# Four paths of low-rank weights per sequence on one core: one visit to z, y, tokens and o per turn of four pairs in place of two visits of two

## The reference

```python
x = x + L0(x)   # x W_base^T + (((x Wt^T) A[e0]^T) B_w[e0]^T) Wp^T * scaling[e0]     e0 of 4, rank 16
x = x + L1(x)   # x W^T + (x A[e1]^T) Bm[e1]^T * scalings[e1]                        e1 of 8, rank 16
x = x + L2(x)   # einsum('bct,bcd->bdt', x, weights[e2]): mixes the 64 tokens        e2 of 8
x = x + L3(x)   # the same with 200 sets of 64x64 weights                            e3 of 200
```

## Time and profile before

| | us |
|---|---|
| median of 3 runs (lowest, highest) | 200.63 (199.47, 202.59) |
| the profiled execution | 200.97 |
| its span, first to last instruction | 199.1 |
| TensorE busy in it | 177.4 |
| the eight turns, from the first z to the end of the last o | 48.7 to 195.6 |

### The profile page before, as it was taken

How to read it: one execution, slowest core, us unless ns; L and a number is a source line. 1 busy time by engine, 2 the same in 40 slices (tenths; PEclk the granted TensorE clock), 3 DMA queues, 4 the chain that set the end, 5 groups by cost and what they waited for, 6 DMA issues and landing times.

```text
span 199.1 us, 7261 instructions
## 1 busy us (share of the span) xinstructions
PE 177.4 (89%) x2304; PEld 140.1 (70%) x2304; DVE 96.8 (49%) x232; ACT 94.2 (47%) x183; POOL 71.7 (36%) x184
## 2 busy tenths in 40 slices
PE   6599898696889699999898989898898989999992
PEld 6377574575668487878686867777686868787781
DVE  1288588629653651746074527524650646154210
ACT  2365742126336645455463636354544545564521
POOL 2525787030653056306521741373056303113000
PEclk9999999999999999999999999999999999999999
DMA  3999412222372846375555737482847375443412
GB/s 80 394 357 289 155 46 87 53 66 72 84 262 71 266 151 198 87 245 164 179 168 173 248 84 229 119 259 78 256 121 229 99 232 169 151 162 82 180 72 89
DMA packets 19081, 32.39 MB, mean 163 GB/s; under 512 B 5878, under 2 KB 5878, under 8 KB 19062
## 3 DMA queue, kind: packets, MB, share of 16 engines
q1 hardware_dynamic: 17744, 31.11, 50.0%
q0 software_dynamic: 1024, 1.05, 1.8%
q10 hardware_dynamic: 294, 0.01, 0.1%
HBM read 22.98 MB, written 9.18 MB: 162 GB/s over the span
## 4 chain that ended last, share of the span: by engine, by line
PE 59%; issue 11%; DVE 9%; ACT 9%; DVEq 6%; DMA 2%; another core or an unknown queue 1%; POOL 0%; SPq 0%; ACTq 0%
PE o_ps L733 35%; PE y_ps L733 8%; PE z_ps L733 5%; DVE y_all L619 4%; PE spare_ps L733 4%; PE p_ps L733 3%; ACT yy L444 3%; DVEq L667 3%; DVEq L657 2%; DMA w_sb<-in_L_cond_W_dram 2%; DVE w_sel L667 2%; ACT z L477 1%; ACT v_sel L458 1%; PE y_ps L745 1%
## 5 line engine op out<-in xcount | busy, mean ns | idle before, releaser
L733 PE MATMUL o_ps<-g,yy 128*128 128x512 f32 x384 | 95.2, 396 | 0.0
L733 PEld LDWEIGHTS o_ps<-g,yy 128*128 128x128 f32 x384 | 70.8, 188 | 16.2
L340 POOL COPY u_sel<-u_tab 128x64 f32 x128 | 28.0, 242 | 89.8 <-PE z_ps L733 70.1
L330 POOL DMA_INDIRECT w_all<-in_L_cond_weights_dram,w_rows x32 | 31.7, 990 | 12.8 <-issue 9.7
L465 ACT ACTIVATE o_sb<-o_ps 128x512 f32<-128x512 f32 x32 | 19.2, 599 | 33.8 <-PE o_ps L733 32.4
L444 ACT ACTIVATE yy<-y_all 128x512 fp32r<-128x512 f32 x32 | 19.6, 635 | 25.4 <-DVE y_all L619 21.5
L633 DVE TENSOR_TENSOR z_sum<-z_ps,z_half 64x128 f32<-64x128 f32 x16 | 4.5, 282 | 50.4 <-ACT z_half L472 50.4
L626 DVE TENSOR_TENSOR yy<-y_all,yy 128x512 fp32r<-128x512 f32 x32 | 20.7, 690 | 2.9 <-ACT yy L444 1.9
L619 DVE COPY y_all<-y_ps 128x512 f32<-128x512 f32 x32 | 20.6, 686 | 0.5
L733 PE MATMUL o_ps<-v_sel,z 128*128 128x512 f32 x64 | 20.1, 394 | 0.0
L733 PE MATMUL z_ps<-y_all,u_sel 128*32 128x64 f32 x512 | 11.6, 222 | 9.4 <-DVE w_sel L667 5.1
(11 more groups left out here) (124 smaller groups left out, 139.8 us busy)
## 6 DMA issues: line engine op xcount, KB each, us to landing
x_raw<-in_x_dram SPq DMA_DIRECT2D x16, 512.0 KB
v_sel<-v_table SPq DMA_DIRECT2D x128, 64.0 KB, 2.1
out_dram<-o_sb SPq DMA_DIRECT2D x14, 512.0 KB, 3.1
w_sb<-in_L_cond_W_dram SPq DMA_DIRECT2D x4, 256.0 KB, 4.8
wb_sb<-in_L_cond_W_base_dram SPq DMA_DIRECT2D x4, 256.0 KB, 6.3
wp_sb<-in_L_cond_Wp_dram SPq DMA_DIRECT2D x2, 512.0 KB, 6.8
wt_sb<-in_L_cond_Wt_dram SPq DMA_DIRECT2D x1, 1024.0 KB
out_dram<-o_sb SPq DMA_DIRECT2D x4, 256.0 KB, 2.8
```

The costliest lines, as they stand in the source:

```text
L330: pool.indirect_dma_start(out=w3_all[:, j, :], out_offset=None, in_=w3_flat, in_offset=bass.IndirectOffsetOnAxis(ap=w3_rows[:, j:j + 1], a ...
L340: nc.gpsimd.tensor_copy(u_sel[u % 2][:, :, b, RANK * part:RANK * part + RANK], u_tab[:, :, bass.ds(e, 1), :].rearrange("p k a r -> p k (a r)")
L733: return nc.tensor.matmul(dst, lhsT, rhs, start=start, stop=stop)
```

## The change

TensorE makes one visit a turn: `reduce(i)` (z of four pairs), `mix()` (y of the four pairs of turn i+1), `token_mix(i+2)`, then four applies. All its waits but those of apply stand at the head: `mix_ready(i+1)`, `token_ready(i+2)`, then those of reduce. y_ps has four banks, y_all, u_sel and z are for four pairs. The keep-warm transposes and three setup products use the new banks of y_ps.

```diff
-        y_ps = ctx.enter_context(nc.psum_tensor("y_ps", [PART, 2, D], F32))
+        y_ps = ctx.enter_context(nc.psum_tensor("y_ps", [PART, QUAD, D], F32))
...
-                 "g01_0": 6, "g01_1": 4, "g01_2": 5, "g01_3": 7}
+                 "g01_0": 6, "g01_1": 4, "g01_2": 5, "g01_3": 1}
```

SyncE, one turn, and GpSimd:

```diff
+            def turn(i, loads=True):
                 if loads:
-                    load(i + 1 + h, 1 - h)
-                for u in range(2 * h, 2 * h + 2):
-                    fetch_v(i + 1, u)
-                store(i, h)
+                    for h in range(2):
+                        load(i + 2, h)
+                for h in range(2):
+                    for u in range(2 * h, 2 * h + 2):
+                        fetch_v(i + 1, u)
+                    store(i, h)
...
-            for u in range(2):
+            for u in range(QUAD):
                 place_u(0, u)
...
+            gather_w3(range(2 * QUAD, 3 * QUAD))
+
+            for i in range(QUADS - 1):
+                if i < QUADS - 3:
+                    pool.wait_ge(w3_plus, i + 3)
+                    gather_w3(range(QUAD * (i + 3), QUAD * (i + 4)))
+
+                pool.wait_ge(z_done, i + 1)
+                for u in range(QUAD):
+                    place_u(i + 1, u)
```

ACT, with V doubled in the turn that uses it:

```diff
+            def turn(i, first=False, ahead=True, more=True):
+                act.wait_ge(z_done, i + 1)
...
+                if ahead and not first:
+                    copy_p(i + 2)
+                for u in range(2):
+                    double_v(i, u)
+                for u in range(QUAD):
+                    copy_out(i, u)
+                    if first and u == 1:
+                        copy_p(1)
+                    if u < 2:
+                        double_v(i, u + 2)
+                    if more and not first:
+                        high_y(i + 1, u)
+                if first:
+                    for u in range(QUAD):
+                        high_y(1, u)
+                    copy_p(2)
...
+            for t in range(KC - 1):
                 read(f"g01_{t}", g01[:, 0, t, :], bank_of(f"g01_{t}"))
             for u in range(2):
                 high_y(0, u)
...
+            read(f"g01_{KC - 1}", g01[:, 0, KC - 1, :], bank_of(f"g01_{KC - 1}"))
+            for u in range(2, QUAD):
+                high_y(0, u)
```

DVE, a turn and the way into the loop:

```diff
+            def turn(i, ahead=True, more=True):
+                sum_z(i)
+                low_z(i)
                 if more:
+                    for u in range(QUAD):
+                        copy_y(i + 1, u)
+                    low_y(i + 1, 0)
+                if ahead:
+                    place_w2(i + 3)
+                    add_w3(i + 3)
+                if more:
+                    for u in range(1, QUAD):
+                        low_y(i + 1, u)
...
+            low_y(0, 1)
+            sum_z(0)
+            low_z(0)
             for u in range(2, QUAD):
                 low_y(0, u)
...
+            for i in range(1, 3):
+                add_w3(i)
+                place_w2(i)
+            for u in range(QUAD):
+                copy_y(1, u)
+            for u in range(QUAD):
+                low_y(1, u)
+            add_w3(3)
+            place_w2(3)
+            with dve.Fori(1, QUADS - 3) as i:
+                turn(i)
```

```diff
+            def turn(i, ahead=True, more=True):
                 if more:
-                    mix(part)
...
+                    mix_ready(i + 1)
+                if ahead:
+                    token_ready(i + 2)
+                reduce(i)
+                if more:
+                    mix()
+                if ahead:
+                    token_mix(i + 2)
+                for u in range(QUAD):
+                    apply(i, u)
...
+            mix_ready(0)
+            mix()
+            for k in range(KC):
+                g01_part(k, KC - 1)
+
+            reduce(0)
+            for u in range(2):
+                apply(0, u, u == 0)
+            token_ready(1)
+            token_mix(1)
+            apply(0, 2)
+            mix_ready(1)
+            mix()
+            token_ready(2)
+            token_mix(2)
+            apply(0, QUAD - 1)
+            with pe.Fori(1, QUADS - 2) as i:
+                turn(i)
+            turn(QUADS - 2, ahead=False)
+            turn(QUADS - 1, ahead=False, more=False)
```

More of the change, by code:

```diff
@@ L85, in build @@
         second.close()
-        u_sel = [sb(f"u_sel{n}", [PART, KC, 2, ZR // 2]) for n in range(2)]
+        u_sel = [sb(f"u_sel{u}", [PART, KC, 2, ZR // 2]) for u in range(QUAD)]
         v_sel = [sb(f"v_sel{u}", [PART, 2, D], F32R) for u in range(QUAD)]
@@ L477, in half @@
                     nc.scalar.activation(z[rows, :, toks], z_sum[rows, :, :], ACT.Copy).then_inc(zh_set, 1)
-                if more:
-                    for u in range(2 * part, 2 * part + 2):
-                        high_y(to, u)
-                if h == 0 and not last:
-                    copy_p(i + 1)
-                copy_out(i, 2 * h)
-                if more:
-                    for u in range(2 * part, 2 * part + 2):
-                        double_v(to, u)
-                copy_out(i, 2 * h + 1)
+                if ahead and not first:
[14 more added lines that the diff above has]
+                    copy_p(2)
             read("u0", u_tab[:, :, 0:E0, :].rearrange("p k e r -> p k (e r)"),
@@ L669, in place_w2 @@
                                               ).then_inc(w2_placed, 1)
-            def half(i, h, ahead=True, more=True):
-                to, part = next_half(i, h)
-                sum_z(i, h)
-                low_z(i, h)
+            def turn(i, ahead=True, more=True):
+                sum_z(i)
+                low_z(i)
                 if more:
-                    for u in range(2 * part, 2 * part + 2):
-                        copy_y(to, u)
-                    for u in range(2 * part, 2 * part + 2):
-                        low_y(to, u)
-                if h == 1 and ahead:
-                    add_w3(i + 2)
-                    place_w2(i + 2)
+                    for u in range(QUAD):
[7 more added lines that the diff above has]
+                        low_y(i + 1, u)
             add_w3(0)
@@ L868, in mix, with apply @@
                                 rows = slice(SEQ * b, SEQ * b + SEQ)
[L869 removed]
+                                last = mm(y_ps[to, u // 2 * 2 + b, col:col + SEQ], x_raw[rows, u, d:d + SEQ], p_now[rows, u, :],
                                           True, True)
                     last.then_inc(y_done, 1)
[L873 removed]
+            def apply(i, u, first=False):
                 n = u % 2
@@ L880, in apply, with reduce @@
                     mm(o_ps[n][:, :], yy[u][:, k, 1, :], g01[:, 0, k, :], False, False)
[L882 removed]
+                pe.wait_ge(zl_set, 2 * (i + 1))
                 pe.wait_ge(v_twice, QUAD * i + u + 1)
[L885 to L898 removed]
+                mm(o_ps[n][:, :], z[:, u, :], v_sel[u][:, 0, :], False, False)
+                mm(o_ps[n][:, :], z[:, u, :], v_sel[u][:, 1, :], False, True).then_inc(o_done, 1)
+            def reduce(i):
+                pe.wait_ge(yf_set, QUAD * (i + 1))
+                pe.wait_ge(u_placed, 4 * QUAD * (i + 1))
+                wait(pe, z_summed, i)
+                for u in range(QUAD):
                     for k in range(KC // 2):
@@ L938, in _ @@
             g01_step(3)
-            mix_ready(0, 0)
-            mix(0)
-            pe.wait_ge(setup_dve, DVE_DONE["g01_3"])
-            for h in range(2):
-                half(0, h, first=True)
-            with pe.Fori(1, QUADS - 1) as i:
-                for h in range(2):
-                    half(i, h)
-            for h in range(2):
-                half(QUADS - 1, h, last=True)
+            mix_ready(0)
[14 more added lines that the diff above has]
+            with pe.Fori(1, QUADS - 2) as i:
+                turn(i)
+            turn(QUADS - 2, ahead=False)
+            turn(QUADS - 1, ahead=False, more=False)
 _INS = ['x', 'itok_B_0_3', 'itok_B_0_6', 'itok_B_0_7', 'itok_B_1_198',
```

167 lines of the change are left out of this document (56 added, 111 removed).

## The result

The changed kernel takes 212.12 us (median of four runs, 211.51 to 212.45) where the kernel before, timed beside it, takes 201.61 (199.47 to 202.87): a ratio of 1.060, 95% interval 1.053 to 1.067. The forecast was 199.5 us, 195.5 to 204.0, most likely no difference. It is slower, and by more than any rival said.

A forecast was written before the change was run, and what follows sets the result against it. TensorE, busy 177.4 of 199.1 us, plus its waits was taken to bound the kernel. Terms of 194.45 us, 2.8 of gather stalls and 0.9 of clock gave span 198.15, run 200.0; forecast 199.5 us, range 195.5 to 204.0.

The forecast's parts named there:

- its stalls (2.8 and 0.4): TensorE stalls going with GpSimd's gathers: 0.7 us in each of four loop turns, 2.8 us, and 0.4 ahead of the loop.
- its clock term: TensorE running slowly after the long idle at turn 1: 0.9 us taken, bounds 0 and 3.5.
- z of turn 1: Start of the second z group, the first loop turn: forecast at 75.8 us, including 0.4 for a gather stall.
- five turns: Steady loop turns with tokens, in the new matmul order: 16.8 us each, 84.0 us in all, without gather stalls.
- the last turn: Turn without y and tokens, to its last V matmul: 14.2 us, including 0.35 us of exposed z chain.
- the hole: TensorE's idle at the handover from turn 0 to turn 1, released by w_sel: 7.3 us.
- z's chain: ScalarE and VectorE work behind z: some 4.3 us from a turn's start, wanted at 6.6, so hidden in steady turns.
- U: Next turn's U, 16 copies in four visits of 1.37 us: starts at about 2 us, done by 8, hidden.
- the head's 0.8 us: z's wait for w_sel at the old loop turn's head, 0.76 to 0.82 us: goes, as token weights are placed earlier.
- rival B: Array clock falls in the handover idle and stays low for 7 us of work: 3.5 us, run 202.6; chance 0.13.
- Rival C, SyncE,: SyncE's queue of V fetches, loads and stores sets turns at 18.0 us under a gather stall: 204.9 us; chance 0.18.
- Rival A: Gather stall falls under o's queued long matmuls instead of short ones, and the clock holds: run 195.8 us; chance 0.27.

The follow-up runs named there:

- quiet profile: Changed kernel, unchanged, profiled on a chip without gather stalls: 197.06 us against 193.24 for the kernel before, ratio 1.019.
- e5: Changed kernel with gathers moved behind y, under o, and three high y and the copy of p before turn 0's last eviction, token weights before low y: 194.61 us, quiet.
- e6: Changed kernel with gathers of pairs 8 to 31 replaced by direct DMAs of other rows (wrong weights): 195.80 us quiet, 193.64 us on a stalling chip.
- e7: Changed kernel with gathers of turns 2 to 7 moved to run under o or into the setup: 197.89 us quiet, 204.84 us stalling.
- e9: Changed kernel with 44 unused transposes on TensorE behind the last V of turn 0: 198.51 us, where the kernel before took 193.15.
- e12: Changed kernel with each gather of the turns made of two direct DMAs, expert's number in a register: 197.54 us, ratio 0.999 to the kernel before.
- e14: e11 with each turn's direct DMAs issued ahead of the wait for z instead of behind y: 188.35 us, ratio 0.942 to the kernel before.
- e8: Changed kernel, gathers moved under o, tokens of turn 1 before the first apply, its y between the first two: 188.59 us, ratio 0.968, quiet.
- e13: Kernel before with each gather of the turns made of two direct DMAs: 217.15 us, a single run, where the kernel before took 199.68.
- e4: Changed kernel, turn gathers replaced by one early DMA of other rows (wrong weights), plus the reordering of e3_handover: 194.94 us, single run.
- e3_timed: The handover kernel: same edit to the changed kernel as e3_handover, timed on a stalling chip: 206.37 us against 200.41 for the kernel before, ratio 1.046.
- e11: The order of e8 with each gather of the turns made of two direct DMAs, standing behind y: 203.84 us, ratio 1.035 to the kernel before.
- e3_handover: Changed kernel with three high y and the copy of p before turn 0's last eviction, token weights before low y: 190.47 us, single run, quiet.

## Why the prediction was wrong, point by point

- **The sum without stalls came near, in part by luck.** Without its stalls (2.8 and 0.4) and its clock term it gives a span of 194.05 us; the quiet profile has 195.4. Term by term: z of turn 1 at 75.4, measured 76.30; five turns 84.0, measured 84.98 (161.28 less 76.30), of which 1.7 is the low clock; turn 6 16.3, measured 16.13; the last turn 14.2, measured 14.5; the end 4.15, measured 3.5. Two errors cancel in the first term. The first z was forecast at 49.3 and came at 51.65, by the fall of the clock in the setup, which no term had: in the two profiles in which the clock held there (e5 and the second e6) it came at 49.19 and 48.99. And the hole was forecast at 7.3 and measured 6.20 and 6.27, with its chain and releaser. z's chain and U stay hidden in the steady turn; in the last turn the second o starts 3.66 us behind the first, for 3.33 elsewhere, the 0.35 us forecast.
- **The step that failed is the price of the gather stalls.** I found their cause by coincidence and priced only what they left in the middle of a turn: 0.8 us a turn, 2.8 for four turns, and 0.4 ahead of the loop, 3.2 in all. Measured against the quiet chip, from the first z on: 16.6 us, 8.18 in turn 0 and 8.45 in turns 1 to 5, with the low clock that they bring. In the loop the price depends little on the order: 1.65 us a turn in the kernel before (18.75 for 17.10), 1.8 to 1.9 in each of three turns of the changed one (18.4 to 18.45 for 16.59). I had taken half of it. Ahead of the loop a stall cost more: 3.5 us in z of turn 0 (4.65 for 1.15) and 2.7 in y of turn 1 (4.7 for 2.0), where the kernel before lost 2.3 in all of turn 0. That this is so because 64 z and 128 y matmuls, one every 0.016 us, stand there with nothing long queued is argued, not shown; what e7 shows is the other side: under o the same gathers cost TensorE nothing at once.
- **The stalls were also in what I called another hole.** Of the head's 0.8 us I said that the change takes it away. It is the second half of those 1.65 us: on quiet chips it isn't there in most turns (0.9 us in all for 5.1). The profile of before could not part the two, since its two turns without gathers are also those behind which no token weights are awaited. So most of the 7.65 us by which I found the old loop too long was no slack of its order (on the quiet chip five turns take 86.57 us, 1.0 more than five times 17.11), and the gain from it was a gain against stalls which came back.
- **The clock was under-priced.** 0.9 us for one fall, bounds 0 and 3.5. There are three falls on the stalling chip and two on the quiet one. The one in the setup and the one behind z of turn 0 (2.5 us, 5.48 for 3.0, of which 0.7 hide a wait for z that the quiet profile has) were not on my list; the latter follows from stalls and not from the handover. The one behind the handover is 1.7 us on a quiet chip (z 1.94 for 1.10; y to tokens 2.77 for 1.92) and about 3.3 here (turn 1 takes 21.6 us, 5.0 over 16.6, of which 1.7 are gaps inside z). The rule of the Trainium skill ("TensorE: Matmul & The Clock Gate", Part 1: the HAM clock gate) that I weighed, that the array's clock falls when it idles, is what e9 and the windows show; it spoke against the change and deserved more than the 0.13 of rival B. My objection to it, that y's 15 to 18 ns may be issue and not the array, does not hold at the low clock: the same y takes 3.58 us at 0.52 and 2.09 at 1.00.
- **Rival C, SyncE,** did not happen in the changed kernel; it happened in e7, where o ran on and SyncE's queue took the stalls. **Rival A** was right that o covers a stall and wrong on where the stalls would lie; the prediction had them within z and y. What it leaned on, that the stall in turn 0 of the kernel before cost little, does not hold: that turn takes 20.92 us for 18.59 on the quiet chip.
- Added up for the stalling chip, spans: 198.15 forecast, 210.5 measured. z of turn 1 came at 83.01 for 75.8: 7.2 us, by 3.5 (z), 2.5 (clock) and 2.7 (y) in turn 0, less 1.5 net: the first z 0.9 later, the hole 1.1 shorter, and the 0.75 of a wait and the 0.4 of a stall that the forecast had there. Turn 1 took 21.6 for 16.8, 4.8 more; the next three 4.9 more in all; from there to the end 0.8 less. That is 16.1, and the sum had set 3.7 aside for stalls and clock: 12.4 remain.

What stays open: what in an indirect DMA stops the queues, why on some chips only, the two gaps of e9, and why a stall costs more in turn 0 than in the loop. That the chips of e12 to e14 would have stalled under gathers is inferred from the time of the kernel before there (196.5 to 204.3), not from a profile. The changed kernel itself was not run beside e6 on the stalling chip; the handover kernel stands for it there.

## What to carry to other kernels

Price a disturbance by whole turns with and without it, not by the gap that it leaves on one engine. Here the gap inside z was 0.5 us, z to y lost 0.86, and the turn lost 1.65: the rest came back as a wait at the next head and looked like slack of the order. Such a stall can be read best on an engine that issues many short instructions (SyncE's eight fetches), since long queued matmuls hide it on another. Ask also what it will meet in the stretches that run once: turn 0 took most of the extra loss. Waits gathered at the head of a turn can make one long idle stretch of several short ones, and that is paid again at the low clock. And before a loop's holes are counted as slack of its order, take away the suspected disturbance once: here most of them went with it. A kernel without gathers in the turns and without the handover's hole took 0.942 of the time of the kernel before where that one stalls; on a quiet chip e8, with gathers and without the hole, took 0.968.

## What the runs showed of the hardware

- Indirect DMAs from GpSimd can hold up the issue of other engines: inside the changed kernel's groups TensorE stood 0.5 to 1.2 us at a time, ending about 1 us behind the last gather of a group; in e7 SyncE's eight fetches took 8.65 us for 5.59, while long matmuls went on; VectorE's first copy of y of turn 1 began 4.0 us behind the first matmul of that y, 1.4 on the quiet chip; and ScalarE resumed with TensorE in the earlier trace rows. Direct DMAs from the same queue at the same places did none of it on the same chip. On the three quiet chips the same gathers stalled nothing that these profiles show.
- TensorE's granted clock fell to 0.50 in each of the stretches of 3.8 to 8.3 us of idling behind the setup (3.84, 4.80 and 5.11 in e13, 4.99 in e4, 5.56 in e7, 6.2 in the changed kernel, 8.34 in e12) and behind 4.65 us of broken work. At 2.5 to 2.9 us it went both ways: e5 (2.49 us idle, then z in 1.42 and y in 3.29), e3_timed (2.91) and three heads of e11 (2.6 to 2.7) fell, e3_handover (2.60) and another head of e11 (2.93) did not. The same holds behind the 1.8 to 2.4 us in the setup: it fell in the changed kernel (2.10 and 2.09) and e3_handover (1.76), and held in the kernel before (2.10), e5 (2.37) and the second e6 (1.77).
- A gather of 128 rows takes GpSimd 1.25 us, one behind the other (0.95 of them busy); two direct DMAs of 64 rows in its place, with the register loads, take 2.28.
